# A mixture-of-experts loop: one rstd instruction and one group of indirect DMAs for two tiles in place of one

## The reference, cut to what matters

```python
tok = x_flat[top_idx]
h = einsum('ecd,edh->ech', tok, W1) + b1
h = layernorm(h) * ln1_g + ln1_b          # over 512 values
h = gelu(h)
out_e = einsum('ech,ehd->ecd', h, W2) + b2
outputs = zeros.at[top_idx].add(out_e * w)
final = layernorm(outputs) * ln_g + ln_b  # over 128 values
x = x + gb * final
```

## Time and profile before

| | us |
|---|---|
| median of 3 runs | 287.15 (286.02 to 287.50) |
| the profiled execution | 288.67 |
| its span | 286.6 |
| PE busy | 254.8 |
| DVE busy | 216.1 |
| POOL busy | 173.8 |
| ACT busy | 157.8 |
| expert loop, first gather to the end of the last scatter's issue | 138.17 to 279.90 |

### The profile page before, as it was taken

How to read it: one execution, slowest core, us unless ns; L and a number is a source line. 1 busy time by engine, 2 the same in 40 slices (tenths; PEclk the granted TensorE clock), 3 DMA queues, 4 the chain that set the end, 5 groups by cost and what they waited for, 6 DMA issues and landing times.

```text
span 286.6 us, 6472 instructions
## 1 busy us (share of the span) xinstructions
PE 254.8 (89%) x1755; PEld 166.5 (58%) x1756; DVE 216.1 (75%) x873; ACT 157.8 (55%) x420; POOL 173.8 (61%) x220
## 2 busy tenths in 40 slices
PE   0998899989989999898999999999999999999640
PEld 0555565689967677554446565655566655566530
DVE  7789996988945999898377877767777777778530
ACT  3669757698513687579134554445454445555410
POOL 6669763000750666410576888888888888886560
PEclk9999999999999999999999999999999999999975
DMA  5940189952929699980232223222222222220000
GB/s 149 243 148 1 34 210 281 269 146 54 239 57 350 190 334 310 286 247 2 69 104 78 74 73 85 83 83 72 73 68 76 84 83 78 73 68 27 19 5 0
DMA packets 47313, 35.29 MB, mean 123 GB/s; under 512 B 4582, under 2 KB 42589, under 8 KB 47162
## 3 DMA queue, kind: packets, MB, share of 16 engines
q1 hardware_dynamic: 42312, 24.71, 31.3%
q0 software_dynamic: 3744, 9.77, 11.9%
q10 hardware_dynamic: 1234, 0.53, 0.8%
HBM read 24.34 MB, written 11.08 MB: 124 GB/s over the span
## 4 chain that ended last, share of the span: by engine, by line
PE 67%; DVE 8%; POOL 6%; DMA 5%; issue 4%; SPq 4%; ACT 3%; POOLq 0%; DVEq 0%; ACTq 0%
PE PS L1535 14%; PE PS L1516 12%; PE PS L1526 8%; PE PS L1520 4%; PE PS L1506 3%; PE PS L1270 3%; DMA BIG<-k_pad 3%; PE PS L1415 2%; PE PS L1411 2%; PE PS L1443 2%; DMA X<-in_L_attn_x_dram 2%; POOL rs L535 2%; PE PS L1537 2%; PE PS L1350 2%; PE PS L1320 2%
## 5 line engine op out<-in xcount | busy, mean ns | idle before, releaser
L820 ACT ACTIVATE V<-PS,gb1T 128x128 f32<-128x128 f32 x156 | 58.6, 456 | 59.5 <-PE PS L1526 58.2
L607 POOL DMA_INDIRECT SBk<-rows,idgi x39 | 41.8, 1072 | 22.8 <-DVE idsi L1186 15.2
L1535 PE MATMUL PS<-BIG,V 128*128 x312 | 47.8, 295 | 0.9 <-DVE Wst L1228 0.9
L616 POOL DMA_INDIRECT out_dram<-Wst,idsi x39 | 39.6, 1017 | 11.1 <-DVE Wst L1239 7.4
L1535 PEld LDWEIGHTS PS<-BIG,V 128*128 128x128 f32 x312 | 44.3, 202 | 3.0 <-issue 1.3
L1222 DVE TENSOR_SCALAR V<-PS,mv,rs 128x512 f32<-128x512 f32 x39 | 31.5, 806 | 18.4 <-POOL rs L626 17.8
L1516 PE MATMUL PS<-BIG,V 128*128 x78 | 40.7, 603 | 2.4 <-issue 1.6
L626 POOL TENSOR_TENSOR rs<-ve,half 128x2 f32<-128x2 f32 x42 | 30.6, 728 | 11.0 <-DVE ve L1243 10.1
L1212 DVE BATCH_NORM_STATS2 st<-PS 128x6 f32<-128x512 f32 x39 | 27.1, 694 | 6.5 <-PE PS L1520 6.0
L1526 PE MATMUL PS<-ident,V 128*128 128x128 f32 x156 | 25.5, 286 | 1.7 <-ACT V L820 1.7
L578 POOL TENSOR_TENSOR Hh<-Hh,outb 128x1024 f32<-128x1024 f32 x4 | 9.5, 2415 | 23.7 <-ACT SBk L733 23.7
(11 more groups left out here) (254 smaller groups left out, 517.6 us busy)
## 6 DMA issues: line engine op xcount, KB each, us to landing
BIG<-k_pad SPq DMA_DIRECT2D x32, 256.0 KB, 5.7
BIG<-in_L_ffn_W_dram SPq DMA_DIRECT2D x1, 2048.0 KB, 9.8
rows<-GL SPq DMA_DIRECT2D x4, 512.0 KB, 4.5
rows<-Hh SPq DMA_DIRECT2D x8, 256.0 KB, 4.6
out_dram<-Hh SPq DMA_DIRECT2D x8, 256.0 KB, 4.4
rows<-U SPq DMA_DIRECT2D x4, 512.0 KB, 4.4
X<-in_L_attn_x_dram SPq DMA_DIRECT2D x3, 512.0 KB, 6.4
Wst<-la_rows SPq DMA_DIRECT2D x1, 1024.0 KB, 5.2
```

The source lines that it names most:

```text
L607: pool.indirect_dma_start(out=XG[:, u, :], out_offset=None, in_=rows, in_offset=bass.IndirectOffsetOnAxis(ap=idgi[:, t:t + 1], axis=0), bo ...
L616: pool.indirect_dma_start(out=out_rows, out_offset=bass.IndirectOffsetOnAxis(ap=idsi[:, t:t + 1], axis=0), in_=FO[:, t % RING, :], in_offs ...
L820: a.activation(AT[:, u, k, :], PS[:, 3, P * k:P * k + P], ACT.Gelu, bias=gb1T[:, 1, bass.ds(e, 1), k], scale=gb1T[:, 0, bass.ds(e, 1), k]) ...
L1535: m.matmul(dst, AT[:, u, k, :], W2s[:, bass.ds(e, 1), k, :].rearrange("p a d -> p (a d)"), start=(k == 0), stop=False)
```

## The change

The tiles are grouped: tile 0 alone, then the pairs (1, 2), (3, 4), ... (35, 36), then 37 and 38 alone. A round r takes the statistics of one group of hidden tiles (a, a + 1) and of the outputs of a group that is four tiles older (a - 4, a - 3), writes one spread of up to four columns, and POOL makes one rstd instruction of them. The outputs of the last six tiles are taken one by one. POOL then issues both gathers of the group, and then both scatters. FO has six places for rows in place of three, XG twelve in place of nine (four of them now lie in BIG, behind the weights). DVE's program is written out for all rounds, without a loop. PE's order of work stays, but its blocks hold 12 tile steps and load 15 registers. What is computed stays.

```diff
-XRING = 3 * RING
+XRING = 12
+PAIRED = range(1, MAX_TILES - 3, 2)
+FRING = 6
...
+        hidden_rounds = [(0,)] + [(t, t + 1) for t in PAIRED] + [(MAX_TILES - 2,), (MAX_TILES - 1,)]
+        out_rounds = [(), (), (0,)] + [(t, t + 1) for t in PAIRED[:-2]] + [(t,) for t in range(PAIRED[-2], MAX_TILES)]
+        hidden_rounds += [()] * (len(out_rounds) - len(hidden_rounds))
+        round_of_hidden = {t: r for r, tiles in enumerate(hidden_rounds) for t in tiles}
+        round_of_out = {t: r for r, tiles in enumerate(out_rounds) for t in tiles}
+
+        def hidden_at(t):
+
+            r = round_of_hidden[t]
+            return r % RING, 2 - len(hidden_rounds[r]) + hidden_rounds[r].index(t)
+
+        def out_at(t):
+
+            r = round_of_out[t]
+            return r % RING, 2 + out_rounds[r].index(t)
+
+        def rstd_columns(r):
+            return r % RING, slice(2 - len(hidden_rounds[r]), 2 + len(out_rounds[r]))
...
             for t in range(AHEAD):
                 gather(t)
-            for t in range(MAX_TILES + RING + 1):
-                if t < MAX_TILES + RING:
-                    pool.wait_ge(s_var1, t + 1)
-                    g.tensor_tensor(rs1[:, t % RING, :], ve1[:, t % RING, :], half[:, 0:2],
-                                    ALU.pow).then_inc(s_rsd1, 1)
-                if t + AHEAD < MAX_TILES:
-                    gather(t + AHEAD)
-                if t > RING:
-                    scatter(t - RING - 1)
+            gathered, scattered = AHEAD, 0
+            for r in range(len(out_rounds)):
+                at, cols = rstd_columns(r)
+                pool.wait_ge(s_var1, r + 1)
+                g.tensor_tensor(rs1[:, at, cols], ve1[:, at, cols], half[:, cols], ALU.pow).then_inc(s_rsd1, 1)
+                while gathered < min(2 * r + 1 + AHEAD, MAX_TILES):
+                    gather(gathered)
+                    gathered += 1
+                ready = sum(len(outs) for outs in out_rounds[:r + 1])
+                last_pairs = r >= len(PAIRED)
+                while scattered < (MAX_TILES if r == len(out_rounds) - 1 else ready - 1 if last_pairs else ready):
+                    scatter(scattered)
+                    scattered += 1
...
-            def expert_step(t, k, rounds=None):
...
+            def hidden_stats(t):
+                dve.wait_ge(s_h, t + 1)
+                return step.mark(v.bn_stats(st1[:, t % RING, 0, :], PS[:, t % RING, :]))
+
+            def hidden_means(t, stats):
+                at, col = hidden_at(t)
+                step.settle(stats)
+                v.memset(tick[:, 0:1], 0.0)
+                return step.mark(v.bn_aggr(mv1[:, at, col, :], st1[:, t % RING, 0, :]))
+
+            def out_stats(t):
+                dve.wait_ge(s_o, t + 1)
+                return step.mark(v.bn_stats(st1[:, t % RING, 1, :], PS[:, 5 + t % RING, 0:D]))
+
+            def out_means(t, stats):
+                at, col = out_at(t)
+                step.settle(stats)
+                v.memset(tick[:, 1:2], 0.0)
+                return step.mark(v.bn_aggr(mv1[:, at, col, :], st1[:, t % RING, 1, :]))
+
+            def hidden_normed(t):
+                at, col = hidden_at(t)
+                dve.wait_ge(s_rsd1, round_of_hidden[t] + 1)
+                if t >= RING:
+                    dve.wait_ge(s_hp, t - RING + 1)
+                v.tensor_scalar(NH[:, t % RING, :], PS[:, t % RING, :], mv1[:, at, col, 0:1], rs1[:, at, col:col + 1],
+                                ALU.subtract, ALU.mult).then_inc(s_nh, 1)
+
+            def out_scaled(t, means):
+                at, col = out_at(t)
+                step.settle(means)
+                if t >= FRING:
+                    dve.wait_ge(s_sc[t % FRING], 16 * (t // FRING))
+                v.scalar_tensor_tensor(FO[:, t % FRING, :], PS[:, 5 + t % RING, 0:D], mv1[:, at, col, 0:1],
+                                       XG[t % XRING][:, 2 * D:3 * D], ALU.subtract, ALU.mult).then_inc(s_fo, 1)
+
+            def out_ready(t):
+                at, col = out_at(t)
+                dve.wait_ge(s_rsd1, round_of_out[t] + 1)
+                dve.wait_ge(s_fo, t + 1)
+                v.scalar_tensor_tensor(FO[:, t % FRING, :], FO[:, t % FRING, :], rs1[:, at, col:col + 1],
+                                       XG[t % XRING][:, D:2 * D], ALU.mult, ALU.add).then_inc(s_f, 1)
+
+            def spread(r, means):
+                at, cols = rstd_columns(r)
+                step.settle(means)
+                v.tensor_scalar(ve1[:, at, cols], mv1[:, at, cols, 1], LN_EPS, None, ALU.add).then_inc(s_var1, 1)
+
+            step.mark(v.memset(mv1[:], 1.0))
+            step.settle()
+
+            def round_step(r):
+
+                hidden = hidden_rounds[r] if r < len(out_rounds) else ()
+                outs = out_rounds[r] if r < len(out_rounds) else ()
+                normed, ready = (hidden_rounds[r - 1], out_rounds[r - 1]) if r else ((), ())
+                next_out = out_rounds[r + 1][0:1] if r + 1 < len(out_rounds) else ()
+                last = None
+                if normed:
+                    hidden_normed(normed[0])
+                if ready:
+                    out_ready(ready[0])
                 if hidden:
-                    dve.wait_ge(s_h, t + 1)
-                    last = v.bn_stats(st1[:, u, 0, :], PS[:, u, :])
-                if rows:
-                    dve.wait_ge(s_o, t - RING + 1)
-                    last = v.bn_stats(st1[:, u, 1, :], PS[:, 5 + u, 0:D])
-                if stats:
-                    step.mark(last)
-                if not static or 1 <= t <= MAX_TILES:
-                    dve.wait_ge(s_rsd1, t)
-                    if not static or t > RING:
-                        dve.wait_ge(s_hp, t - RING)
-                    v.tensor_scalar(NH[:, w, :], PS[:, w, :], mv1[:, w, 0, 0:1], rs1[:, w, 0:1],
-                                    ALU.subtract, ALU.mult).then_inc(s_nh, 1)
-                token = XG[:, (k - RING - 1) % XRING]
-                if final:
-                    if rounds is not None:
-                        dve.wait_ge(s_sc[w], 16 * rounds)
-                    v.scalar_tensor_tensor(FO[:, w, :], PS[:, 5 + w, 0:D], mv1[:, w, 1, 0:1], token[:, 2 * D:3 * D],
-                                           ALU.subtract, ALU.mult).then_inc(s_fo, 1)
-                if stats:
-                    step.settle()
-                    v.memset(tick[:, 0:1], 0.0)
-                    for q in (0, 1)[pairs]:
-                        last = v.bn_aggr(mv1[:, u, q, :], st1[:, u, q, :])
-                    step.mark(last)
-                if final:
-                    dve.wait_ge(s_rsd1, t)
-                    dve.wait_ge(s_fo, t - RING)
-                    v.scalar_tensor_tensor(FO[:, w, :], FO[:, w, :], rs1[:, w, 1:2], token[:, D:2 * D],
-                                           ALU.mult, ALU.add).then_inc(s_f, 1)
-                if stats:
-                    step.settle()
-                    v.tensor_scalar(ve1[:, u, pairs], mv1[:, u, pairs, 1], LN_EPS, None, ALU.add).then_inc(s_var1, 1)
-
-            step.mark(v.memset(ve1[:], 1.0))
-            step.settle()
-
-            def rounds_at(t):
-                done = (t - RING - 1) // RING
-                return done if done > 0 else None
-
-            for t in range(XRING):
-                expert_step(t, t, rounds_at(t))
-            with nc.vector.Fori(1, MAX_TILES // XRING) as c:
-                step.enter(c - 1, 2 * XRING)
-                for k in range(XRING):
-                    expert_step(XRING * c + k, k, RING * c + k // RING - (1 if k % RING else 2))
-                step.leave(MAX_TILES // XRING - 1)
-            for t in range(MAX_TILES // XRING * XRING, MAX_TILES + RING + 1):
-                expert_step(t, t % XRING, rounds_at(t))
+                    stats = hidden_stats(hidden[0])
+                if len(ready) == 2:
+                    out_ready(ready[1])
+                if hidden:
+                    last = hidden_means(hidden[0], stats)
+                if len(outs) == 2:
+                    out = out_stats(outs[1])
+                if len(normed) == 2:
+                    hidden_normed(normed[1])
+                if len(outs) == 2:
+                    out = last = out_means(outs[1], out)
+                if len(hidden) == 2:
+                    stats = hidden_stats(hidden[1])
+                if len(outs) == 2:
+                    out_scaled(outs[1], out)
+                if len(hidden) == 2:
+                    last = hidden_means(hidden[1], stats)
+                if hidden or outs:
+                    spread(r, last)
+                for t in next_out:
+                    out = out_means(t, out_stats(t))
+                    out_scaled(t, out)
+
+            for r in range(len(out_rounds) + 1):
+                round_step(r)
...
-                regs = [pe.alloc_register(f"experts_{name}{q}") for q in range(4 * RING)]
```

(36 more changed lines are left out.)

2 lines of the change are left out of this document (1 added, 1 removed).

## The result

Over 20 executions each, the changed kernel takes 288.06 us at the median (286.27 to 290.45) and the kernel before 286.97 (285.69 to 287.92). The ratio is 1.0038 with a 95% interval of 1.0020 to 1.0056: no gain, and a loss of some 1 us within the 0.5% that counts as no change. I had forecast 284.5 in a range of 282.6 to 287.1. In all runs of this text, executions more than 1.5% above the fastest of their kernel count in no ratio but do count in the medians; three of them took 301, 305 and 815 us.

What follows compares the result with a forecast made beforehand. POOL, at 3.34 us a tile, was taken to bound tiles 12 to 34. Relieving it gave -4.2, one head fewer -0.5, the start +1.8, the end +0.25: -2.65 from 287.15, so 284.5, range 282.6 to 287.1.

Steps and rivals of the forecast that it cites:

- the round: POOL's rstd, two gathers and two scatters for a pair of tiles: 6.29 us against 6.68 before.
- the rstd of four columns: On POOL, one rstd instruction per pair: 1.03 us, priced from a four-column rstd elsewhere in the kernel.
- a second gather: On POOL, a gather right behind another: a gap of 0.31 us and 1.00 us for the gather.
- The two engines are nearly level: In the expert loop, POOL and PE each need 6.29 us a pair, PE's share of block heads included.
- The stall at turn(1): PE waits for DVE, which takes tile 0's output before normalising hidden tile 1: 1.8 us lost once.
- L1239 (L1268 after) beneath gathers: DVE's two-input instruction contending with POOL's gathers: taken at nothing, at worst 2 x 0.35 us a pair.
- 2 x 0.53: PE's two block heads with register loads, at tiles 12 and 24, between T(1) and T(34): 0.53 us each.
- sum by PE: Start of turn(34) on PE: 152.64 + 33 x 3.10 + 2 x 0.53 = 256.0, where it was 258.94.
- behind it the loop runs as now: After turn(34), the last tiles take as long as before, apart from 0.25 us to the last scatter.
- the 0.25 of the longer list: At the end, the last spread stands behind one more instruction of 0.27: +0.25 us to the last scatter.
- rival 3: PE's clock falls in the 1.8 us stall at turn(1), costing 1.75 us: 286.2, no change; chance 0.09.
- Rival 4: At the end, PE's clock stays high over the last downs, 1.75 us less: 282.8; or start loses less; chance 0.12.
- Rivals 1 and 2: POOL: 1, round still sets the pace, 285.7 to 287.1, chance 0.15; 2, contention or longer round, 288.6 to 293.4, chance 0.09.

Runs made afterwards that it cites:

- experiment 11: Changed kernel with tile 0's output taken by DVE in round 2, rows of 16 expert numbers and PE's loop written out: 282.88 us, ratio 0.9866 to kernel before.
- experiment 7: The changed kernel run and profiled again with no edit, beside the kernel before: 288.75 us, ratio 1.0030.
- experiment 3: Kernel before with rows of 15 expert numbers and 15 registers loaded at each block head in place of 12: 303.40 us, ratio 1.0536.
- experiment 5: Changed kernel with rows of 16 expert numbers in place of 15, all 16 loaded at each block head: 286.51 us, ratio 0.9974 to kernel before.
- experiment 6: Kernel before with its 12 registers, rows of expert numbers 13 apart in place of 12: 294.87 us, ratio 1.0284.
- experiment 2: Changed kernel with PE's expert loop written out, 15 registers still loaded per block: 287.01 us, ratio 0.9977 to kernel before.
- experiment 1: Changed kernel with DVE taking tile 0's output in round 2, not at the end of round 1: 286.27 us, ratio 0.9939 to kernel before.
- experiment 10: Changed kernel with tile 0's output taken in round 2 and rows of 16 expert numbers: 284.44 us, ratio 0.9890 to kernel before.
- experiment 9: Changed kernel with three useless 128x512 products on PE between down(0) and turn(1), in the stall: 287.99 us, ratio 1.0025 to kernel before.

## Why the prediction was wrong

**What held.** POOL was what bounded tiles 12 to 34, and the pairs take it off the path: the round is 6.28 (forecast 6.29), the rstd of four columns 1.04 (1.03), a second gather 1.02 (1.00). PE then runs at 3.10 a tile with no wait inside the rounds. The two engines are nearly level, as I had said: even with the short heads of experiment 11 the last full rstd lets L1253's instruction end 0.6 us before PE needs it. The stall at turn(1) is 1.72 (1.8), at the place and by the cause given. Four-column rounds have no hidden price, and neither has L1239 (L1268 after) beneath gathers: both gathers of a round have one beneath them and stay at 1.07 and 1.02.

**The step that failed** is the term "2 x 0.53" of the sum by PE, together with "behind it the loop runs as now". I took the price of a head from the earlier trace rows, a load of 12 registers, and applied it to a load of 15; the change's own description says 15, and I passed over it. The heads at tiles 12 and 24 measure 1.24 and 1.51 over a usual tile, that at 36 0.76 over the old tile 36. A smaller error lies in the same term: I priced every head by the first, and the trace of before already has the head inside the loop dearer (tiles 9 and 18):

```profile
173.49 1.12 PE L1516 MATMUL PS<-BIG,V 128*128 x2 [0.30 <-issue]
...
203.50 1.12 PE L1516 MATMUL PS<-BIG,V 128*128 x2 [0.63 <-issue]
```

Here is the sum again, from the second profile of the changed kernel (experiment 7), whose clock at the end of the loop is low as in the profile of before:

| stretch | before | changed | difference | forecast |
|---|---|---|---|---|
| T(0) to T(1) | 3.37 | 5.16 | +1.8 | +1.8 |
| T(1) to T(34) | 108.09 | 105.15 | -2.9 | -4.7 |
| T(34) to T(38) | 11.98 | 12.75 | +0.8 | 0 |
| T(38) to the last scatter | 8.01 | 8.35 | +0.3 | +0.25 |

The sum is 0.0 where I had -2.65. The missing 1.8 of the second row are the two heads (0.73 and 0.99 over the 0.53 that I had), and the 0.8 of the third the last one. The last row decides nothing: in the seven profiles whose clock falls at the end of the loop, of both kernels and their variants, it is 7.9 to 8.5, so I can't tell the 0.25 of the longer list from the moment of that fall. The experiments settle the cause: a row of 60 bytes costs about 0.24 for each of its last three numbers (0.73 at tile 36 in experiment 3; experiment 5 takes 0.48 off by adding a sixteenth). It isn't that the rows of experiment 5 start on 64 bytes: 12 registers take 3.44 at tile 36 from byte 576 and 3.46 from byte 624 (experiment 6). The loop costs another 0.23, 0.62 and 0.27 (experiment 2), but not because its body is longer: with 15 registers tile 36 takes 4.18 behind the loop of nine steps (experiment 3) and 4.20 behind that of 12.

**The rest is rival 3,** to which I gave 0.09. The clock does fall behind the stall in a part of the executions. It was seen in two of the six profiles that have the stall unfilled, costs 1.5 to 1.6 us there, and goes away with the stall (experiments 1, 10 and 11) or with work in it (experiment 9). A mean clock of 0.974 or less, as one of the two profiles with both falls has it (0.972; the other has 0.975), comes in 22 of the 78 executions that have the stall and count in a ratio, and in none of the 35 without it or with work in it. An execution whose clock fell only behind the stall can't be told by its mean from one where it fell only at the end, so how often it falls stays open, and with it how much of the 1.1 us at the median is this; experiment 1 puts it at 1.0, give or take 0.8. I priced it at 1.75, near the 1.5 to 1.6 measured, and set its chance by one stretch of one trace. The Trainium skill (TensorE: Matmul & The Clock Gate, Part 1) says that the clock follows how busy the engine has lately been and that the moment of a change varies from run to run. The runs fit that, with the same 1.7 us stall followed by 1.00 in two profiles of the unedited changed kernel and by 0.50 in the third.

**Rival 4 explains the profile.** In the profiled execution of the changed kernel the clock stayed high over the last downs, and T(38) to the last scatter took 7.02 in place of 8.35 (experiment 7). That is 1.3 us by which the changed kernel differs from itself, and the mean clocks of the kernel before (0.977 to 0.985) vary in the same way. The lower end of my range should have been this rival's 282.8, not 282.6; nothing hangs on it. Comparing that one profile with the one of before would have shown a gain of 1.7 us where the medians have a loss of 1.1.

Rivals 1 and 2 (0.24 together) were wrong: POOL was never late for PE. My uncertainty sat on POOL, where the prices were sound, and none of it on PE's list, which I took as unchanged because its instructions were.

## What to carry to other kernels

A change that lengthens a table of which an engine loads a row at the head of each block has a price there, even if the instructions of the body stay: price the load anew, by the row's size and start, and the heads at the entry, inside and behind a loop each by itself. Where an engine works off its list with no slack, look at the first and last rounds of a regrouped order by themselves; one output taken too early cost 1.8 us here, and 1.5 to 1.6 more through the clock in a part of the executions. And when a stall as long as this one of 1.7 us is made on PE, count on the clock falling in a part of the executions: compare medians of many executions, not two profiles.

## What the runs showed that I had not expected

A load of registers from SBUF costs by how the numbers lie. With rows that start and end on 16 bytes, a head stands idle 0.2 to 0.7 us for 12 registers and 0.4 to 0.8 for 16, its share of the loop included (0.2 to 0.3 for 16 with the loop written out). With the row's start off 16 bytes 12 registers take 2.4 to 2.6 us and 15 take 3.1 to 3.3, some 0.2 us a register. With a good start and three numbers over (15), tile 36 takes 0.73 more than with 12, which is 0.24 for each of the three; 16 take 0.27 more than 12. The Trainium skill (Runtime: NRT & Kernel Launch, Instruction fetch mechanics) says that a load of registers, which its launch sequence makes from HBM, takes about 200 ns for each register even in bulk. It has no figure for a load from SBUF. The rows off 16 bytes come to about the same (2.60 / 12 = 0.22); the aligned ones do not: 12 of them cost at most 0.7 in all. That the unit is four numbers is my reading of these five cases; other lengths were not tried, nor was the absolute place of the table in SBUF.
